# GpSimd centres half of the tiles of a 30-step recurrence, and a constant row carries their bias

## The reference, cut to what matters

```python
def step(h, _):
    h = h + 0.01 * jnp.tanh(h)
    h = h * jax.nn.sigmoid(h)
    h = _layernorm(h, ln_w, ln_b)
    h = jnp.einsum('bsc,dc->bsd', h, W) + b
    return (h, None)
x, _ = jax.lax.scan(step, x, None, length=30)
```

## Time and profile before

| | |
|---|---|
| Median of three runs | 1304.41 us |
| The profiled execution's own time | 1303.05 us |
| Its span, first to last instruction | 1301.1 us |
| TensorE busy share of the span | 98% |
| VectorE | 89% |
| ScalarE | 74% |
| GpSimd | 58% |
| Mean granted TensorE clock | 0.997 of full speed |

### The profile page before, as it was taken

How to read it: one execution, slowest core, us unless ns; L and a number is a source line. 1 busy time by engine, 2 the same in 40 slices (tenths; PEclk the granted TensorE clock), 3 DMA queues, 4 the chain that set the end, 5 groups by cost and what they waited for, 6 DMA issues and landing times.

```text
span 1301.1 us, 30193 instructions
## 1 busy us (share of the span) xinstructions
PE 1269.5 (98%) x9788; PEld 1150.9 (88%) x9788; DVE 1163.0 (89%) x3032; ACT 961.4 (74%) x1169; POOL 755.8 (58%) x787
## 2 busy tenths in 40 slices
PE   8899999999999999699999999999999999999998
PEld 7677777777777777599999999999999999999998
DVE  7888888888888877899999999999999999999996
ACT  2455555555555555799999999999999999999994
POOL 3455555455555554666666666666666666666664
PEclk9999999999999999899999999999999999999999
DMA  6111111111111000000000000000000000000004
GB/s 191 41 42 46 58 55 44 40 40 40 40 40 40 0 1 1 1 2 1 0 0 0 0 0 0 0 0 0 0 0 0 0 0 0 0 0 0 0 0 129
DMA packets 29810, 27.74 MB, mean 21 GB/s; under 512 B 3285, under 2 KB 21464, under 8 KB 29656
## 3 DMA queue, kind: packets, MB, share of 16 engines
q1 hardware_dynamic: 29784, 27.41, 6.6%
HBM read 23.21 MB, written 4.19 MB: 21 GB/s over the span
## 4 chain that ended last, share of the span: by engine, by line
PE 83%; DVE 10%; ACT 3%; issue 2%; POOL 0%; DMA 0%; SPq 0%; DVEq 0%; ACTq 0%
PE psum L867 33%; PE psum L909 16%; PE psum L884 8%; PE psum L652 4%; PE psum L654 4%; PE psum L653 4%; PE psum L823 4%; PE psum L674 3%; PE psum L669 3%; DVE emb_n L1465 2%; DVE xh_mem L1253 1%; PE psum L663 1%; ACT emb_f L1017 1%; PE psum L683 1%; DVE upd L1431 1%
## 5 line engine op out<-in xcount | busy, mean ns | idle before, releaser
L511 POOL TENSOR_TENSOR h_ring<-g_ring,f_rs 128x512 f32<-128x512 f32 x480 | 485.9, 1043 | 256.7 <-DVE f_rs L1358 256.6
L867 PE MATMUL psum<-w_t,y_all 128*128 128x128 f32 x3840 | 467.6, 275 | 0.0
L867 PEld LDWEIGHTS psum<-w_t,y_all 128*128 128x128 f32 x3840 | 448.0, 192 | 0.0
L1270 DVE BATCH_NORM_STATS2 f_stat<-g_ring 128x6 f32<-128x256 f32 x960 | 393.3, 423 | 2.4 <-ACT g_ring L966 2.4
L909 PE MATMUL psum<-ident,h_ring 128*128 128x128 f32 x1920 | 359.5, 273 | 3.2 <-POOL h_ring L511 2.8
L1287 DVE SCALAR_TENSOR_TENSOR u_ring<-t_ring,psum 128x1024 f32<-128x1024 f32 x232 | 283.3, 1221 | 32.3 <-ACT t_ring L976 27.7
L976 ACT ACTIVATE t_ring<-psum 128x1024 f32<-128x1024 f32 x232 | 238.0, 1026 | 53.7 <-PE psum L867 49.6
L909 PEld LDWEIGHTS psum<-ident,h_ring 128*128 128x128 f32 x1920 | 251.4, 142 | 15.8 <-POOL h_ring L511 3.6
L884 PE MATMUL psum<-bias,ones_bf 65*128 65x256 bf16 x960 | 262.1, 274 | 1.1 <-DVE u_ring L1287 1.1
L980 ACT ACTIVATE y_all<-psum 128x1024 f32<-128x1024 f32 x240 | 243.6, 1015 | 14.6 <-PE psum L909 14.6
L966 ACT ACTIVATE g_ring<-u_ring 128x1024 f32<-128x1024 f32 x240 | 251.6, 1049 | 1.9 <-DVE u_ring L1287 1.6
(11 more groups left out here) (191 smaller groups left out, 1990.5 us busy)
## 6 DMA issues: line engine op xcount, KB each, us to landing
work<-in_adj_dram SPq DMA_DIRECT2D x16, 1024.0 KB, 5.4
x_tok<-in_x_dram SPq DMA_DIRECT2D x16, 256.0 KB, 5.6
out_dram<-y_all SPq DMA_DIRECT2D x7, 512.0 KB, 3.2
work<-in_L_gnn_conv_w_dram SPq DMA_DIRECT2D x1, 1088.0 KB
out_dram<-y_all SPq DMA_DIRECT2D x2, 256.0 KB, 3.3
work<-in_L_gnn_w_ih_dram SPq DMA_DIRECT2D x1, 384.0 KB
work<-in_L_gnn_w_hh_dram SPq DMA_DIRECT2D x1, 192.0 KB
work<-in_L_gnn_W_dram SPq DMA_DIRECT2D x1, 64.0 KB, 5.2
```

Source lines behind the costliest of these rows:

```text
L511: pool.tensor_tensor(tiles(h_ring[j % 4])[:, NT * h:NT * h + NT, :], tiles(g_ring[j])[:, NT * h:NT * h + NT, :], spread(f_rs[:, both(j), a ...
L867: m = pe.matmul(y_ps[k % 2][:, h, C * t:C * t + C], y_all[:, GT * k + NT * h + t, :], w1_t[:], start=False, stop=True, skip_group_check=True)
L1270: ins = dve.bn_stats(f_stat[:, j % 4, 0, 2 * q:2 * q + 2, :].rearrange("p t w -> p (t w)"), two)
```

## The change

In each half of four tiles, the first two (`PLAIN = 2`) stay as they were: GpSimd multiplies them by the reciprocal root, in one instruction of 256 columns instead of one of 512. The last two are centred on GpSimd: for each tile one tensor-scalar adds the negative mean and multiplies by the reciprocal root, both read per partition from SBUF. The negative means of two groups come from one more small GpSimd instruction per pair of groups (`less_mean`, four slots after the sum).

A centred tile's 128 channels add to zero, so its last channel need not be kept. TensorE transposes only 127 channels of such a tile; the 128th row of its place in PSUM holds ones, written once by `ones_row` ahead of the recurrence, and is copied along into `y_all`. Its weight `w1c_t` has the last input channel's weights subtracted from the others and the bias in the last row. So these tiles need no bias matmul, and `bias` is called twice a slot instead of four times. In set-up, VectorE builds that weight with two more instructions and copies fewer bias rows, TensorE transposes it, and ScalarE copies it out. `f_stat` grows so that each group has its own statistics.

```diff
+            def less_mean(j, s):
+                pool.wait_ge(f_bn, s + 2)
+                settle(pool, s_passed_pool)
+                pool.tensor_scalar(f_less[:, j:j + 2, :], f_stat[:, j:j + 2, 0, :, 1], -1.0, 1.0,
+                                   ALU.mult, ALU.mult).then_inc(f_mean, 1)
...
             def scale(i, j, s):
...
+                pool.wait_ge(f_mean, i * (GROUPS // 2) + j // 2 + 1)
                 wait(pool, f_turn, s - 3)
                 for h in (j % 2, 1 - j % 2):
-                    at = GT * (j % 2) + NT * h
-                    pool.tensor_tensor(tiles(h_ring[j % 4])[:, NT * h:NT * h + NT, :], tiles(g_ring[j])[:, NT * h:NT * h + NT, :],
-                                       spread(f_rs[:, both(j), at:at + NT], NT, C), ALU.mult).then_inc(f_norm, 1)
+                    first = NT * h
+                    at = GT * (j % 2)
+                    pool.tensor_tensor(tiles(h_ring[j % 4])[:, first:first + PLAIN, :], tiles(g_ring[j])[:, first:first + PLAIN, :],
+                                       spread(f_rs[:, both(j), at + first:at + first + PLAIN], PLAIN, C), ALU.mult)
+                    for t in range(first + PLAIN, first + NT):
+                        ins = pool.tensor_scalar(tiles(h_ring[j % 4])[:, t, :], tiles(g_ring[j])[:, t, :],
+                                                 f_less[:, j, t:t + 1], f_rs[:, both(j), at + t:at + t + 1], ALU.add, ALU.mult)
+                    ins.then_inc(f_norm, 1)
...
             def slot(it, k):
+                older = earlier(it, k, LAG_M)
+                if older is not None and k % 2 == 0:
+                    less_mean(*older[1:])
...
-                        m = pe.matmul(y_ps[k % 2][:, h, C * t:C * t + C], y_all[:, GT * k + NT * h + t, :], w1_t[:],
-                                      start=False, stop=True, skip_group_check=True)
+                        m = pe.matmul(y_ps[k % 2][:, h, C * t:C * t + C], y_all[:, GT * k + NT * h + t, :],
+                                      w1_t[:] if t < PLAIN else w1c_t[:], start=False, stop=True, skip_group_check=True)
...
-            def bias(k, part):
-                h, c = part // 2, part % 2
-                pe.matmul(y_ps[(k + 1) % 2][:, h, 2 * C * c:2 * C * c + 2 * C], ones_bf[:],
-                          bias1[:, 0:2, :].rearrange("p t c -> p (t c)"),
-                          start=(c == 0), stop=False, skip_group_check=True)
+            def bias(k, h):
+                pe.matmul(y_ps[(k + 1) % 2][:, h, 0:PLAIN * C], ones_bf[:],
+                          bias1[:, 0:PLAIN, :].rearrange("p t c -> p (t c)"),
+                          start=True, stop=False, skip_group_check=True)
+
+            def ones_row(b):
+                for t in range(0, NT, NT - PLAIN):
+                    pe.matmul(bank[b][:, C * t:C * t + C * (NT - PLAIN)], ones_bf[:],
+                              bias1[:, PLAIN:NT, :].rearrange("p t c -> p (t c)"), start=(t == 0), stop=True,
+                              skip_group_check=True)
...
-                        m = pe.transpose(g_ps[j % 2][:, t // NT, P * (t % NT):P * (t % NT) + P],
-                                         tiles(h_ring[j % 4])[:, t, :], ident[:])
-                    if ahead and n % 2 == 0:
-                        if n == 0:
+                        rows = P if t % NT < PLAIN else P - 1
+                        m = pe.transpose(g_ps[j % 2][0:rows, t // NT, P * (t % NT):P * (t % NT) + P],
+                                         tiles(h_ring[j % 4])[:, t, 0:rows], ident[:])
+                    if ahead and n % NT == 1:
+                        if n == 1:
                             bias_free(it, k)
-                        bias(k, n // 2)
+                        bias(k, n // NT)
...
+                act.activation(w1c_t[:], bank[CONV + (FILLS - 1) % 4][:, 2 * C:3 * C], ACT.Copy)
...
+                dve.wait_ge(s_wturn0, 1)
+                link(dve.tensor_scalar(nat[:, N_W0, :], w1_nat, w1_nat[:, C - 1:C], None, ALU.subtract))
+                dve.tensor_copy(nat[:, N_W0, C - 1:C], vec(FB1))
...
-                for t in range(NT):
+                for t in range(PLAIN):
                     for r in range(3):
                         dve.tensor_copy(bias1[32 * r:32 * r + 1, t, :], part_bf[32 * r:32 * r + 1, r, :])
```

More of the change, by code:

```diff
@@ L46 @@
 LAG_S = 1
+LAG_M = 4
 LAG_P = 5
@@ L55 @@
 EARLY = 7
+PLAIN = 2
 SEED_SLOPE = -0.5
@@ L103, in build @@
         w1_t = sb("w1_t", [P, C])
+        w1c_t = sb("w1c_t", [P, C])
         ident = sb("ident", [P, P])
@@ L107, in build @@
         half_neg = sb("half_neg", [P, 8])
-        f_stat = sb("f_stat", [P, 4, 2, GT, 3])
+        f_stat = sb("f_stat", [P, GROUPS, 2, GT, 3])
         f_var = sb("f_var", [P, BY_POWER, GT])
         f_rs = sb("f_rs", [P, 2, PAIR])
+        f_less = sb("f_less", [P, GROUPS, GT])
         f_share = sb("f_share", [P, PAIR])
@@ L153, in build @@
         emb_bias = gates[0:1, 8 * P + 7 * C:8 * P + 7 * C + NSE]
-        part_bf = sba("part_bf", [KB, 3, C], BF16)
+        part_bf = gates[0:KB, 8 * P + 3 * C:8 * P + 3 * C + 3 * C // 2].bitcast(BF16).rearrange("p (r c) -> p r c", c=C)
         bcol = sba("bcol", [P, 32])
@@ L297, in build @@
         f_bn = sem("f_bn")
+        f_mean = sem("f_mean")
         f_v = sem("f_v")
@@ L561, in step @@
                     power(3)
+                    less_mean(2, 2)
                 if l1:
@@ L573, in step @@
                     power(0)
+                    less_mean(0, 0)
                     scale(0, 0, 0)
@@ L619, in turn_weights @@
                     wait(pe, s_wlow, f - 3)
-                    for i in range(4 if f < FILLS - 1 else 2):
+                    for i in range(4 if f < FILLS - 1 else 3):
                         k = 4 * f + i
@@ L623, in turn_weights @@
                         if f == FILLS - 1:
-                            src = nat[:, (N_W1, N_MSG)[i], :]
+                            src = nat[:, (N_W1, N_MSG, N_W0)[i], :]
                         elif k < TAPS:
@@ L894, in slot @@
                     i, j, s = before
-                    pe.wait_ge(f_norm, 2 * s + 1)
-                    if ends(i, 0) and j < 2:
-                        pe.wait_ge(*((s_conv_pre, B) if j == 0 else (s_r, B)))
+                    if ends(i, 0) and j == 0:
+                        pe.wait_ge(s_conv_pre, B)
+                        ones_row(CONV)
+                        pe.wait_ge(s_x_nmp_lo, B)
+                        ones_row(CHAN)
+                    elif ends(i, 0) and j == 1:
+                        pe.wait_ge(s_r, B)
+                        ones_row(DIST_A)
                     else:
                         pe.wait_ge(f_state, s - 1)
+                    pe.wait_ge(f_norm, 2 * s + 1)
                 for n in range(GT):
@@ L903, in slot @@
                             pe.wait_ge(f_norm, 2 * s + 2)
[L904 to L907, removed]
+                            wait(pe, f_state, s)
                         t = (n + NT * (j % 2)) % GT
-                        m = pe.transpose(g_ps[j % 2][:, t // NT, P * (t % NT):P * (t % NT) + P],
-                                         tiles(h_ring[j % 4])[:, t, :], ident[:])
-                    if ahead and n % 2 == 0:
-                        if n == 0:
+                        rows = P if t % NT < PLAIN else P - 1
[3 more added lines that the diff above has]
+                        if n == 1:
                             bias_free(it, k)
-                        bias(k, n // 2)
+                        bias(k, n // NT)
                 if before is not None:
@@ L1127, in _ @@
             dve.memset(ones_bf[:], 1.0)
-            dve.memset(bias1[:], 0.0)
+            link(dve.memset(bias1[:], 0.0))
+            dve.memset(bias1[0:1, PLAIN:NT, :], 1.0)
             dve.memset(b1_cols, 0.0)
@@ L1269, in statistics_of @@
                 two = g_ring[j][:, 2 * C * q:2 * C * q + 2 * C].rearrange("p (o c) -> p c o", o=2)
-                ins = dve.bn_stats(f_stat[:, j % 4, 0, 2 * q:2 * q + 2, :].rearrange("p t w -> p (t w)"), two)
+                ins = dve.bn_stats(f_stat[:, j, 0, 2 * q:2 * q + 2, :].rearrange("p t w -> p (t w)"), two)
                 if q == GT // 2 - 1:
@@ L1308, in variance @@
                 dve.wait_ge(f_bn, j + 1)
-                squares = f_stat[:, j % 4, :, :, 2].rearrange("p o t -> p t o")
+                squares = f_stat[:, j, :, :, 2].rearrange("p o t -> p t o")
                 dve.tensor_reduce(f_var[:, j, :], squares, AX_X, ALU.add).then_inc(f_v, 1)
@@ L1338, in root_link @@
                         dve.wait_ge(s_z, B)
-                    squares = f_stat[:, j % 4:j % 4 + 2, :, :, 2].rearrange("p g o t -> p g t o")
+                    squares = f_stat[:, j:j + 2, :, :, 2].rearrange("p g o t -> p g t o")
                     dve.tensor_reduce(root[:, VAR, :].rearrange("p (g t) -> p g t", t=GT), squares, AX_X, ALU.add).then_inc(f_link, 1)
```

## The result

The changed kernel takes **1289.8 us** (median of four runs, 1288.97 to 1290.16), against 1303.9 us for the kernel before (median of four): a ratio of **0.989**, 95% interval 0.9873 to 0.9907. It is faster by 14 us, where 47 were forecast. The direction and the range held; the size did not. It lies nearest the rival that had GpSimd late but not the end of it (1284 us).

The account below looks back on a forecast made before the run. TensorE's instruction count (28 at 0.1111 us) was taken to bound the recurrence at 3.11 us a slot. With T = 2.91: 1303.05 - 46.9 (full slots) - 1.2 (last slots) + 1 (ahead) = 1256 us, range 1248 to 1292.

Parts of the forecast that it names:

- the rival that had GpSimd late but not the end of it: Recurrence: tensor-scalar of 0.36 to 0.465, TensorE waits for the first group's second half; 1284 us at 0.43; chance 0.13.
- the T of 2.91: Recurrence: forecast pitch in us a slot, taken where three limits meet at 2.89.
- The rival of VectorE at its busy share: Recurrence: VectorE's 2.97 us a slot is real need and stops the pitch there; 1270 us; chance 0.07.
- The lower bound: GpSimd's tensor-scalar: about 0.26 in a stream, from a 128x128 instruction reading one tensor that took 0.292.
- b: First group, link to link through two GpSimd halves of length h: 9.2 + 2h within 4T; 2.89 at h = 1.18.
- c: Second group, without the odd slot but with four halves and the means: 6.4 + 4h within 4T; 2.78 at 1.18.
- Condition (a): GpSimd's own work: 2T at least 4h + 0.22 + 0.16, the last the release delay; 2.55 at h = 1.18.
- The sign named for lateness: Recurrence trace: TensorE idle before the transposes with GpSimd as the releaser would show GpSimd late.
- Contention at nothing in the recurrence: Recurrence: GpSimd multiplies took 1037 to 1042 ns whatever VectorE did, so contention was costed at nothing.
- The +1 us ahead of the recurrence: Ahead of the recurrence: set-up instructions and four longer hand-over halves, taken as +1 us, between 0 and 2.
- GpSimd as the bound: Recurrence: dear tensor-scalars make GpSimd the bound and the kernel slower, 1460 us at 0.64, 1330 at 0.50; chance 0.12.
- turning point of 1.49 a half: GpSimd's half length at which conditions (a) and (c) break at today's 3.11 pitch, a tensor-scalar of 0.465 us.

Follow-up runs that it names:

- the saving alone: Changed kernel with GpSimd as before the change (one 512-column multiply a half, no means), TensorE as changed: 1253.9 us, ratio 0.9619.
- the relieved even half: Changed kernel with the first half of every even group back in its former form (one 512-column multiply, two bias pieces): 1269.6 us, ratio 0.9736.
- the odd half: Changed kernel with the half of every odd group that is scaled first back in its former form: 1296.9 us, ratio 0.9948.
- the run with constants: Changed kernel with constants (-0.05, 0.1) for both scalars of the tensor-scalars: 1277.8 us, ratio 0.98.
- 1.60 a half (1341 us): Changed kernel with only the mean a constant (-0.05), the reciprocal root still read per partition: 1341.4 us, ratio 1.0295.
- the price without its saving: Changed kernel with each of the two bias pieces issued twice, so TensorE has 28 instructions a slot again: 1305.3 us, ratio 1.0009.

## Why the prediction was wrong in size

**The bound, and the pieces taken away: right.** Every instruction costs 0.111, and VectorE keeps up at 2.91 a slot, under its busy 2.97: 1253.9 us with the saving alone, at the T of 2.91 that the sum had. The rival of VectorE at its busy share falls with that run.

**GpSimd's price: the term that failed.** The tensor-scalar was taken at 0.31 within bounds of 0.26 and 0.43; it is 0.425, at the upper end. The multiply was taken at 0.56 and is 0.60. The half is 1.445 in place of 1.18. Of the 0.265 between them the two tensor-scalars make 0.23. The step behind the choice was that a two-column instruction costs 0.192 with one operand or two, so two small reads more should cost little. That row compares a tensor-tensor with a tensor-scalar of constants and says nothing about scalars read per partition; those go with 72 and 82 ns more length in this form. The lower bound failed as well: with no scalar read the spacing is 0.37, not 0.26. How much of the 0.425 is reads therefore stays open. The range held because it reached past the upper bound's 1284 us, not because the chosen price was right.

The Trainium skill, GPSIMD Engine Reference, section 7, gives some 102 cycles for each small read command, by estimate 0.085 us at the page's clock; the prediction worked 0.43 and 1284 us out of it and set it aside. The lengths of add-then-multiply agree with that estimate (72 and 82 ns a scalar); the spacing with one constant and the single multiply at 607 ns do not.

**The conditions: b and c right in form.** With the measured half and a release of 0.39, which the prediction had at 0.31, they ask for 3.04 and 3.05, and the pitch is 3.054: 231 x (3.113 - 3.054) = 13.6 us of the 14 measured. At the forecast half of 1.18 and the same release b would ask for 2.91. They also gave 1269.6 us within the 1266 to 1271 expected for the relieved even half, and the direction of the odd half once its displaced piece is counted. They hold to some 0.02: b asks for 3.03 where the run with constants measured 3.008. Condition (a) counted the release's delay for every pair, which GpSimd pays only where it waits. The sign named for lateness, TensorE idle before the transposes with GpSimd as the releaser, is what the waits show.

**Contention at nothing in the recurrence: borne out** by the price without its saving, which changed nothing at 3.113, and by GpSimd's lengths, the same at 3.113 and 3.054. **The +1 us ahead of the recurrence** is nearer 2: TensorE's first product starts at 546.41 us before and at 546.02 after the change, but the third at 557.72 and 559.74. Between them TensorE waits 4.60 us for GpSimd's tensor-scalars, where it had waited 2.85 for the multiply, and the product behind that wait runs at a granted clock of 0.50, 1.2 GHz (16 instructions in 3.41 us, against 1.79 for the same product before the change, at 1.00). With 2 in place of 1, and the last slots' 1.2 as forecast, the profiled executions close: 1303.05 - 13.6 - 1.2 + 2 = 1290.2, against 1290.16.

**GpSimd as the bound** did not come at 0.425, but does at 1.60 a half (1341 us) and above. Its turning point of 1.49 a half was not tried; by the prediction's own conditions at 3.11 the first breaks at 1.46 and the third at 1.51, and 1.49 is the middle.

## What to carry to other kernels

When the engine that bounds a loop is relieved, price the engine that takes the work as a latency in the loop's cycle, release to release, and not only as a total: the same relief of GpSimd gained 20 us at one place in the order of halves and lost 7 at the other, where a bias piece also fell behind the wait. An instruction form that the trace has not shown is to be taken near its upper bound, not at the nearest row that leaves a part of it out, and read from start to start once a run has it. And a busy share on TensorE near 99% (595.49 of 600 us) can cover 5% of idle time (0.165 of 3.054 us a slot); instructions times their spacing does not.

## What the runs showed of the hardware that was not expected

On GpSimd, a tensor-scalar over 128 by 128 float32 elements takes 454 ns as add-multiply with two per-partition scalars, 457 as multiply-add, 607 as a single multiply with one scalar, and 793 and 833 in the two runs with subtract-multiply. In the stream these stand 0.425, 0.425, 0.575 and, in both last runs, 0.77 us apart. Adding a negated scalar in place of subtracting it is worth some 300 us in this kernel (1289.8 against one execution of 1597.5). With a constant for one or both scalars it is shorter, 372 and 300 ns, but the next instruction then starts some 0.07 us after its end in place of 0.03 before it: 0.45 apart with one constant, further than the 0.425 with two scalars, and 0.37 with two constants. Why is not shown.
